# Attention probabilities scaled on ScalarE in place of VectorE

## The reference

```python
scores = jnp.einsum('ehd,ehd->eh', q[src], k[dst])
smax = jax.ops.segment_max(scores, src, num_segments=N)
ex = jnp.exp(scores - smax[src])
denom = jax.ops.segment_sum(ex, src, num_segments=N)
attn = ex / denom[src]
out = jax.ops.segment_sum(attn[:, :, None] * v[dst], src, num_segments=N)
...
x = x + out.reshape(N, D) @ wo + bo
```

## Time and profile before

| | |
|---|---|
| median of 2 runs | 1870.9 us (1869.83 to 1871.98) |
| profiled execution, its own time | 1871.84 us |
| span of its trace | 1870.1 us |
| TensorE matmul busy | 1810.0 us (97%) |
| TensorE weight loads busy | 1575.5 us (84%) |
| VectorE busy | 1382.6 us (74%) |
| ScalarE busy | 826.5 us (44%) |
| GpSimd busy | 453.8 us (24%) |
| `normalise`'s product, L1281 | 160 instructions, 150.1 us |

### The profile page before, as it was taken

One profiled execution on the slowest core, in us unless ns is written; L12 is line 12 of the kernel. 1 busy time (PEld: TensorE's weight loads), 2 busy tenths in 40 slices (PEclk: granted clock), 3 DMA queues, 4 the chain that ended last, 5 costly groups with the idle time before them and its releaser, 6 DMA issues. The chain is left out here.

```text
span 1870.1 us, 33910 instructions
## 1 busy us (share of the span) xinstructions
PE 1810.0 (97%) x11814; PEld 1575.5 (84%) x11814; DVE 1382.6 (74%) x2847; ACT 826.5 (44%) x1613; POOL 453.8 (24%) x547
## 2 busy tenths in 40 slices
PE   6988999999999999999999999999999999999999
PEld 4656988999789889998898899988998999887877
DVE  8996668888875588888754988888549888885431
ACT  1552465555432255554322545544226545536220
POOL 2000333112341341113413411125134111262000
PEclk9999999999999999999999999999999999999999
DMA  4213462110300111113011211040112110522001
GB/s 143 55 41 79 141 176 91 38 43 27 123 24 34 58 42 39 38 31 124 4 54 42 58 38 38 27 128 1 46 50 61 38 38 27 142 72 55 1 1 55
DMA packets 50755, 108.43 MB, mean 58 GB/s; under 512 B 18170, under 2 KB 18222, under 8 KB 50640
## 3 DMA queue, kind: packets, MB, share of 16 engines
q1 hardware_dynamic: 50608, 106.87, 19.7%
q0 software_dynamic: 32, 0.03, 0.0%
HBM read 83.62 MB, written 23.25 MB: 57 GB/s over the span
## 5 line engine op out<-in xcount | busy, mean ns | idle before, releaser
L876 ACT ACTIVATE PT<-ps 125x500 fp32r<-125x500 f32 (+1 forms) x480 | 214.3, 520 | 315.1 <-PE ps L1790 315.1
L1690 PE MATMUL ps<-PT,V 125*128 125x250 f32 x2400 | 313.2, 284 | 1.7 <-DVE PT L1288 1.7
L1690 PE MATMUL ps<-kT,qg 128*125 128x512 f32 (+1 forms) x1440 | 302.1, 354 | 6.3 <-DVE nmx L1272 5.6
L1690 PEld LDWEIGHTS ps<-kT,qg 128*125 128x125 f32 x1440 | 245.4, 186 | 56.0 <-issue 6.9
L1690 PEld LDWEIGHTS ps<-PT,V 125*128 125x128 f32 x2400 | 289.6, 190 | 2.9 <-DVE PT L1288 2.9
L1288 DVE TENSOR_TENSOR PT<-ps,PT 125x500 fp32r<-125x500 f32 (+1 forms) x480 | 253.1, 582 | 2.1 <-ACT PT L876 1.7
L1272 DVE CUSTOM_DVE_ANT_0 SB<-ps,bt 125x1250 f32<-125x1250 f32 x140 | 203.9, 1457 | 47.4 <-PE ps L1690 44.6
L1790 PE MATMUL ps<-ident,pbuf 125*125 125x125 f32 x1600 | 202.2, 273 | 9.9 <-DVE PT L1288 4.0
L1790 PEld LDWEIGHTS ps<-ident,pbuf 125*125 125x125 f32 x1600 | 187.2, 189 | 13.6 <-issue 8.8
L870 ACT ACTIVATE pbuf<-SB,nmx 125x1250 f32<-125x1250 f32 x140 | 188.1, 1344 | 12.1 <-DVE nmx L1272 10.4
L1281 DVE TENSOR_SCALAR pbuf<-pbuf,rden 125x1250 f32<-125x1250 f32 x160 | 150.1, 938 | 5.6
(11 more groups left out here) (246 smaller groups left out, 2811.6 us busy)
## 6 DMA issues: line engine op xcount, KB each, us to landing
bt<-edge_bias_scratch SPq DMA_DIRECT2D x40, 546.9 KB
q_scratch<-qc SPq DMA_DIRECT2D x16, 500.0 KB, 2.6
qc<-q_scratch SPq DMA_DIRECT2D x16, 500.0 KB, 4.8
counts_scratch<-cblk SPq DMA_DIRECT2D x10, 546.9 KB
c_rows<-counts_scratch SPq DMA_DIRECT2D x10, 546.9 KB
edge_bias_scratch<-b_rows SPq DMA_DIRECT2D x10, 546.9 KB
counts<-counts_scratch SPq DMA_DIRECT2D x10, 546.9 KB
wm<-in_L_gnn_wo_dram SPq DMA_DIRECT2D x4, 1024.0 KB, 8.6
```

What stands on the lines that cost most here:

```text
L876: sc.activation(PT[:, h % 2, 0, a:b, u * T:(u + 1) * T], ps_T[0:T, i, 0:(b - a) * T].rearrange("p (t n) -> p t n", n=T), ACT.Copy).then_in ...
L1690: e = mm(out_, lhs(a), rhs(b), start=start and i == 0, stop=stop and i == 2)
```

## The change

The product of the probabilities with the reciprocal moves from VectorE to ScalarE. `normalise` on VectorE ends with the reciprocal, which signals `rden`; a new function `scale_unit` on ScalarE waits for `rden` and multiplies `P` in place, by a Copy activation with a per-row scale, and signals `P`. It is called behind each `exp_unit`; in `attn_begin` both of the first two exponentials come ahead of the first two scalings. In the changed kernel's numbering `score_max` is L1283, the two small instructions are L1288 and L1290, `turn_low` is L1297, `out_low` is L1303, `scale_unit` is L876, `turn_out` is L881 and `attn_out` is L886.

```diff
@@ on ScalarE @@
+            def scale_unit(U, u):
+
+                act.wait_ge(s["rden"], U + 1)
+                sc.activation(P[:, u, :], P[:, u, :], ACT.Copy, scale=rden[:, u:u + 1]).then_inc(s["P"], 1)
+
...
             def unit(G, k, last):
                 turn_out(UNITS * G + k, k // 2, k % 2)
                 exp_unit(UNITS * G + k + 2, k % 2, not (last and k == 4))
+                scale_unit(UNITS * G + k + 2, k % 2)
 
             def attn_begin(U):
 
                 exp_unit(U, 0, False)
                 exp_unit(U + 1, 1, False)
+                scale_unit(U, 0)
+                scale_unit(U + 1, 1)
                 turn_out(U, 0, 0)
                 turn_out(U + 1, 0, 1)
                 exp_unit(U + 2, 0)
+                scale_unit(U + 2, 0)
                 exp_unit(U + 3, 1, False)
+                scale_unit(U + 3, 1)
...
                 turn_out(U + 6, 3, 0)
                 exp_unit(U + 7, 1, False)
+                scale_unit(U + 7, 1)
                 rsqrt0(norm)
                 attn_out(G, 2)
@@ on VectorE, in normalise @@
                 v.reciprocal(rden[:, u:u + 1], dmx[:, u:u + 1]).then_inc(s["rden"], 1)
-                dve.wait_ge(s["rden"], U + 1)
-                v.tensor_scalar(P[:, u, :], P[:, u, :], rden[:, u:u + 1], None, ALU.mult).then_inc(s["P"], 1)
```

## The result

The changed kernel takes 1899.6 us (median of 2 runs, 1899.15 to 1900.02) against 1870.9 before: the ratio is 1.0154, with a 95% interval of 1.0137 to 1.0170. It is slower by 1.5%, 28.7 us. The profiled execution took 1899.15 us with a span of 1897.4, which is 27.3 more than the span before.

The account below looks back on a forecast made before the run. TensorE was taken to bound the kernel, at 4.57 us a unit. Added delays of 13.9 (beginning), 5.4 (middle) and 6.4 (end) sum to 25.7 us, taking the profiled 1871.84 to 1897.5; median forecast 1897 us, range 1875 to 1915.

Parts of the forecast that it names:

- The instruction: Each of 160 scalings on ScalarE lasts 1.34 us and takes a place of 1.25 in its queue.
- The middle: Middle of each layer's attention: TensorE loses 0.45 us in each of three middle blocks, 1.35 a layer, 5.4 in all.
- the ring: Waits between VectorE and ScalarE around a pair of units: 9.69 us against TensorE's 9.14, each further pair adding 0.55.
- The beginning: Start of each layer's attention: late scalings delay transposes and scores, 3.8 us in three layers, 2.5 in layer 0, 13.9 in all.
- its other wait: Layer 0's second transposes wait for VectorE's other work ahead of the low halves, hiding 1.3 us of ScalarE's delay.
- The end: End of each layer's attention: last transposes 1.1 us late, the norm behind them 1.6 late, 6.4 in all.
- All else moves along: End of a layer: what follows the 1.6 us delay shifts with it, at no further cost.
- VectorE's relief is worth nothing: Middle of a layer: VectorE's 7.0 us less work in a block gains zero, since TensorE is already busy all 42.00.
- hidden load, by occupancy: Rival: ScalarE has room, 33.5 of 42 us with the scalings, so nothing waits: 1871 us, 1867 to 1878; chance 0.08.
- The slower ring: Rival: longer scalings or handovers make a pair's excess 0.9 us, each block stalls twice: 1911 to 1928; chance 0.17.
- The profile after: VectorE's busy time 150 us lower, ScalarE's 214 higher; layer 1's first transposes 1.5 late, each layer's last 1.1 late.
- signs of being wrong: ScalarE scaling before the second exponential, an instruction not lasting 1.34 us, or TensorE's own pace in the attention changing.

Follow-up runs that it names:

- experiment 1: Changed kernel with attn_out ahead of the scaling on ScalarE after an odd unit, instead of behind it: 1885.3 us, ratio 1.0082.
- experiment 4: Changed kernel with attn_out ahead of the scaling, and units 0 to 3 and the last two of each layer scaled on VectorE: 1867.7 us, ratio 0.9991.
- experiment 2: Changed kernel with the scaling taking a constant in place of the reciprocal, so it waits only for its own exponential: 1872.2 us, ratio 1.0015.
- experiment 7: Experiment 4 with unit 3 and the last unit on ScalarE, rsqrt0 ahead of the last scaling, last reciprocal ahead of turn_low: 1865.0 us, ratio 0.9967.

## Why the prediction was right

The forecast was 1897 us, the measured time is 1899.6. By its own steps:

- *The instruction*: 1.34 forecast, 1.339 measured, 160 of them. ScalarE's queue place of 1.25 holds: two scalings in a row take 2.55 (654.79), and what follows starts 1.24 after a scaling.
- *The middle*: the ring was put at 9.69 and is 9.67; each link is within 0.05. 5.4 forecast, 5.7 measured, 0.45 at the stall shown above. Layer 0 lost less, 1.0: the prediction has TensorE never wait in the middle of the kernel before, but its layer 0 has a wait of 0.18 us there (306.63 us), and the middle of that layer is 0.4 shorter in experiments 1 and 4. Experiments 1 and 2 confirm the cause from two sides: taking `attn_out` out of the ring and taking the reciprocal out each leave ScalarE's load as it is and remove the stalls of the middle.
- *The beginning*: 3.8 forecast for layers 1 to 3, 3.4 to 3.7 measured. The forecast times of layer 1, moved by its 6.08, are met within 0.5: first transposes 656.23 (656.21), second 659.6 (659.57), scores of unit 5 669.6 (670.06), of unit 7 680.4 (680.29). In layer 0 I had put 2.5, since its other wait would hide 1.3, and it is 4.4. This term was mis-sized: the ten transposes take 2.44 and the scores behind them 2.48, in place of 1.32 and 1.98 in layer 1, which is the halved clock, 1.6 us. The 2.8 that remain are near the 2.5.
- *The end*: 1.6 forecast, 1.62 measured in each layer. "All else moves along" was wrong in layers 1 and 3, by 1.5 each, again the clock.
- *VectorE's relief is worth nothing*: shown by experiment 4 for the middle. At the two ends of a layer experiment 7 gains something, 0.55 and 0.3 to 0.7, but with other orders too, so how much of that is VectorE's relief isn't shown.
- *The rivals*: hidden load, by occupancy, falls by experiment 2 (with ScalarE's load kept and the wait removed the time is 1872) and by experiment 4 (136 scalings cost nothing in the right order). It is true that ScalarE had room, and the loss came from where in its queue the instruction stood. The slower ring, from 0.86 late on for a first pair, didn't come: from `dmx` to the scaling it is 0.39 again (814.04 to 814.43), and from `attn_out` to `out_low` 0.40 where 0.41 was read before.
- *The profile after*: VectorE's busy time was to fall by 150 and ScalarE's to rise by 214; they moved by 139.5 and 199.1, since those were sums of durations and the merged times count overlaps once. The last transposes of layer 1 come 1.0 later than before, measured from the first scores and less what beginning and middle added; 1.1 was forecast. One of its signs of being wrong did come: TensorE's own pace changed, at the three stretches of the lower clock.

The errors of the sum offset one another: 4.7 us for the clock in three places were missing, and so were 2.8 us given back outside the attention, 1.6 of it one halving fewer in the last MLP. The terms of the waits were right by themselves (25.4 without the clock, against 25.7); that the clock and what was given back nearly cancel is luck. The total is 1.6 us off in the span and 2.6 in the median, since in the changed kernel the profiled execution lies 0.4 below the median and not 0.9 above.

## What to carry to other kernels

An engine at half its time can still be the wrong place for an instruction: add up the ring that it closes (each wait from one engine to the other and back, each instruction that stands behind it in the queue), and compare that with the pace of the engine that sets the time. Here 0.53 us too much in a ring of 9.67 and two ends of a loop made 1.5%, and moving one unrelated instruction ahead of the new one took back nearly half of that. In this kernel the latency of a step counted in full at the beginning and the end of a layer, and in its middle only what exceeded the slack; so the best split I found is different at each.

## What the runs showed of the hardware that I had not expected

TensorE's granted clock fell from 2.4 to 1.2 GHz for 3.41 us at a time, after TensorE had stood idle for 1.2 to 3.1 us shortly before. A last `attend` then took 5.13 us in place of 3.59. So a delay of 1.6 us cost 1.5 again, in two of four layers that are alike to 0.1 us up to there. Such an idle time isn't always followed by the lower clock: behind the wait of 2.02 us in the last MLP it fell in the kernel before (1679.67), and behind the same wait of 2.01 in the changed kernel it didn't (1707.01). What decides it these runs don't show. The Trainium skill, "ScalarE: Activation LUTs", section "What ACT_TABLE_LOAD costs", gives 93 ns of overlap between activations; the trace is near that: what follows a scaling of 1.34 us starts 1.24 after it (810.14 to 811.38), an overlap of 0.10, and two scalings in a row take 2.55, an overlap of 0.13. Where a scaling has to wait for its reciprocal, ScalarE idles instead, 0.42 us each time in the middle of a layer.
